# Cross attention: where four strip transposes, the scratch results and the values stand in PSUM and on TensorE's queue

## The reference

```python
q = _split_heads(query @ Wq.T + bq)
k = _split_heads(key @ Wk.T + bk)
v = _split_heads(value @ Wv.T + bv)
scores = jnp.einsum('bhqd,bhkd->bhqk', q, k) * scale
scores = jnp.where(mask == 0, NEG_INF, scores)
probs = jax.nn.softmax(scores, axis=-1)
out = jnp.einsum('bhqk,bhkd->bhqd', probs, v)
out = out.transpose(0, 2, 1, 3).reshape(query.shape[0], -1, D_MODEL)
return out @ Wo.T + bo
...
x = _layernorm(x + _L0_xattn_ref(x, ctx_1024, ctx_1024, mask_1x1xSxS2_ik0, ...), axis=-1)
```

## Time and profile before

| what | value |
|---|---|
| median of 3 executions | 491.06 us (490.84 to 491.5) |
| the profiled execution | 491.28 us |
| its span, first to last instruction | 489.5 us |
| TensorE matmuls busy | 439.8 us, 90% |
| TensorE weight loads busy | 308.6 us, 63% |
| VectorE busy | 248.3 us, 51% |
| ScalarE busy | 197.5 us, 40% |

### The profile page before, as it was taken

How to read it: one execution, slowest core, us unless ns; L and a number is a source line. 1 busy time by engine, 2 the same in 40 slices (tenths; PEclk the granted TensorE clock), 3 DMA queues, 4 the chain that set the end, 5 groups by cost and what they waited for, 6 DMA issues and landing times.

```text
span 489.5 us, 9697 instructions
## 1 busy us (share of the span) xinstructions
PE 439.8 (90%) x3440; PEld 308.6 (63%) x3441; DVE 248.3 (51%) x736; ACT 197.5 (40%) x582; POOL 42.4 (9%) x65
## 2 busy tenths in 40 slices
PE   5999999999999879999999999999879989999910
PEld 2797887977878646666666666666655646555500
DVE  0376465564655736566565655656644622222225
ACT  2235335243352426665565656566742110111200
POOL 3001011011010110001010101000000230000043
PEclk9999999999999989999999999999999999999975
DMA  7940000004200040404040406400000020111123
GB/s 282 307 192 1 11 1 11 11 0 161 73 1 2 1 161 0 153 11 149 14 161 1 162 2 248 172 0 2 4 1 1 23 75 0 32 43 43 37 65 103
DMA packets 15192, 33.28 MB, mean 68 GB/s; under 512 B 2128, under 2 KB 9536, under 8 KB 13760
## 3 DMA queue, kind: packets, MB, share of 16 engines
q1 hardware_dynamic: 14384, 30.91, 18.1%
q0 software_dynamic: 768, 1.84, 1.3%
HBM read 26.97 MB, written 5.77 MB: 67 GB/s over the span
## 4 chain that ended last, share of the span: by engine, by line
PE 75%; issue 8%; DVE 5%; ACT 5%; POOL 3%; DMA 3%; POOLq 0%; DVEq 0%; SPq 0%; ACTq 0%
PE bank L416 11%; PE bank L598 7%; PE bank L410 6%; PE bank L475 5%; PE bank L614 5%; PE bank L581 4%; PE bank L499 4%; PE bank L505 4%; PE bank L801 3%; ACT pT L947 3%; PE bank L825 3%; PE bank L807 3%; PE bank L433 3%; PE bank L461 3%; PE bank L734 3%
## 5 line engine op out<-in xcount | busy, mean ns | idle before, releaser
L1168 DVE CUSTOM_DVE_ANT_0 p<-bank,mask 112x375 f32<-112x375 f32 x128 | 63.6, 544 | 32.9 <-PE bank L581 32.1
L940 ACT ACTIVATE p<-p,nm 112x375 f32<-112x375 f32 x128 | 74.8, 606 | 9.7 <-DVE nm L1168 9.0
L598 PE MATMUL bank<-ident,p 112*125 112x112 f32 x384 | 61.1, 285 | 7.7 <-ACT pT L947 6.7
L598 PEld LDWEIGHTS bank<-ident,p 112*125 112x125 f32 x384 | 48.7, 188 | 29.7 <-issue 18.4
L416 PE MATMUL bank<-arena 128*128 128x112 f32 x512 | 61.9, 275 | 0.0
L947 ACT ACTIVATE pT<-bank 125x336 f32<-125x336 f32 x96 | 42.7, 446 | 46.7 <-PE bank L598 46.4
L416 PEld LDWEIGHTS bank<-arena 128*128 128x128 f32 x512 | 59.5, 192 | 0.5 <-issue 0.5
L884 ACT ACTIVATE arena<-bank,nm 112x112 f32<-112x112 f32 x128 | 43.5, 366 | 26.7 <-DVE nm L1043 26.7
L1036 DVE TENSOR_SCALAR arena<-bank 128x448 f32<-128x448 f32 x32 | 20.0, 624 | 41.1 <-PE bank L416 41.1
L410 PE MATMUL bank<-arena 128*112 128x512 f32 x64 | 32.6, 639 | 5.5 <-DMA arena<-in_wqkv 5.5
L892 ACT ACTIVATE arena<-bank 128x448 f32<-128x448 f32 x16 | 8.7, 543 | 58.6 <-PE bank L461 58.6
(11 more groups left out here) (136 smaller groups left out, 590.2 us busy)
## 6 DMA issues: line engine op xcount, KB each, us to landing
arena<-in_ug SPq DMA_DIRECT2D x8, 1024.0 KB, 6.0
arena<-in_dn SPq DMA_DIRECT2D x8, 512.0 KB, 6.9
mid<-in_ctxT SPq DMA_DIRECT2D x8, 375.0 KB, 3.1
arena<-in_wqkv SPq DMA_DIRECT2D x2, 1024.0 KB, 8.6
slots_x<-zeros SPq DMA_DIRECT2D x14, 128.0 KB, 1.8
xs<-slots_x SPq DMA_DIRECT2D x9, 128.0 KB, 2.0
slots_y<-p SPq DMA_DIRECT2D x9, 128.0 KB, 1.7
arena<-in_wqkv SPq DMA_DIRECT2D x2, 512.0 KB, 4.4
```

The source lines that it names most:

```text
L598: mm = pe.transpose(PE_T2[i % 2][0:SK, t * S:(t + 1) * S], p2[i % RING][:, t * SK:(t + 1) * SK], ident[0:S, 0:S])
L940: act.activation(p2[i % RING], p2[i % RING], ACT.Exp, bias=nm2[:, i % H:i % H + 1], scale=-1.0).then_inc(exp2, 1)
L1168: v.tensor_tensor_reduce(p2[i % RING], PE_S2[r][0:S, 0:S2], bias[:], 1.0, 3e38, ALU.add, ALU.min, accum_out=nm2[:, i % H:i % H + 1]).then_ ...
```

## The change

The transposed strips get four banks in place of two: strip 0 goes to bank 4, strip 1 to bank 7, strip 2 to bank 0 and strip 3 to bank 1. Banks 0 and 1 hold scores of the current slot, so these two wait for the minimum of the strip that was there (`max2`), and the next `score2` waits until both copies are made (`pt2_act`, `pt2_dve`). The scratch results of place 0 (x1's transposes, the queries, the output's two transposes) go to bank 6, in turn with the keys and the output projection; the waits that keep bank 6 apart are in `between`. The scratch results of place 1 go to bank 2 (`PE_L2`) behind the third minimum, and the first third of the next batch's values, before at place 2 in bank 6, joins them. `value2(n - 2)` moves behind `between(n, 2)` and so stands directly ahead of the next scores. In the end of the stage the last `value2` comes ahead of the router's first product.

```diff
-        PE_S2, PE_T2, PE_V2, PE_M2 = bank[0:STRIPS], (bank[4], bank[7]), bank[5], bank[6]
+        PE_S2, PE_V2, PE_M2 = bank[0:STRIPS], bank[5], bank[6]
+        PE_T2 = (bank[4], bank[7], PE_S2[0], PE_S2[1])
+        PE_L2 = PE_S2[2]
...
-            def turn_x1(b, M=PE_S2[0]):
+            def turn_x1(b, M=PE_M2):
...
-            def project_q(b, M=PE_S2[0]):
+            def project_q(b, M=PE_M2):
...
             def turn2_(n, r):
                 pe.wait_ge(exp2, n * STRIPS + r + 1)
-                if r >= 2:
-                    pe.wait_ge(pt2_act, n * 3 + r - 1)
-                elif n == 0:
+                if n == 0 and r < 2:
                     pe.wait_ge(y1, B)
                     pe.wait_ge(pt1, 4 * B)
                 elif r == 0:
-                    pe.wait_ge(pt2_act, n * 3)
-                else:
-                    pe.wait_ge(pt2_dve, n)
+                    pe.wait_ge(pt2_act, n * 3 - 2)
+                elif r == 1:
+                    pe.wait_ge(pt2_act, n * 3 - 1)
+                elif n + 1 < SLOTS:
+                    pe.wait_ge(max2, (n + 1) * STRIPS + r - 1)
...
-            def turn_o(b, M=PE_S2[0]):
+            def turn_o(b, M=PE_M2):
...
-            def turn_on(b, M=PE_S2[0]):
+            def turn_on(b, M=PE_M2):
...
-            def turn_x2(b, M=PE_S2[1]):
+            def turn_x2(b, M=PE_L2):
...
                 b, g = n // GROUPS, n % GROUPS
-                if place < 2:
-                    pe.wait_ge(max2, n * STRIPS + 1 + place)
+                if place == 1:
+                    pe.wait_ge(max2, n * STRIPS + 3)
                 if (g, place) == (0, 0) and b + 1 < B:
+                    if b == 0:
+                        pe.wait_ge(ot1[1], B)
+                    if b >= 2:
+                        pe.wait_ge(y2, b - 1)
                     turn_x1(b + 1)
                 if (g, place) == (0, 1) and b >= 1:
-                    project_v(2, b, PE_S2[1])
+                    project_v(2, b, PE_L2)
                 if (g, place) == (0, 2) and b + 1 < B:
-                    if b == 0:
-                        pe.wait_ge(ot1[1], B)
-                    elif b >= 2:
-                        pe.wait_ge(y2, b - 1)
+                    pe.wait_ge(x1t_sb, b + 2)
                     project_k(0, b + 1)
                 if (g, place) == (1, 0) and b + 1 < B:
+                    pe.wait_ge(k_sb, (b + 1) * KC + 1)
                     project_q(b + 1)
                 if (g, place) == (1, 1) and b >= 2:
                     turn_x2(b - 2)
                 if (g, place) == (1, 2) and b + 1 < B:
-                    pe.wait_ge(k_sb, (b + 1) * KC + 1)
+                    pe.wait_ge(q_sb, b + 2)
                     project_k(1, b + 1)
                 if (g, place) == (2, 0) and b >= 1:
+                    if b + 1 < B:
+                        pe.wait_ge(k_sb, (b + 2) * KC)
+                    else:
+                        pe.wait_ge(y2, B - 2)
                     turn_o(b - 1)
-                if (g, place) == (2, 2) and b + 1 < B:
-                    pe.wait_ge(k_sb, (b + 2) * KC)
-                    project_v(0, b + 1)
+                if (g, place) == (2, 1) and b + 1 < B:
+                    project_v(0, b + 1, PE_L2)
                 if (g, place) == (3, 0) and b >= 1:
                     turn_on(b - 1)
                 if (g, place) == (3, 1) and b + 1 < B:
-                    project_v(1, b + 1, PE_S2[1])
+                    project_v(1, b + 1, PE_L2)
                 if (g, place) == (3, 2) and b >= 1:
-                    if b + 1 < B:
-                        pe.wait_ge(v_sb, (b + 1) * KT + 1)
-                    else:
-                        pe.wait_ge(y2, B - 2)
                     out2(b - 1)
...
+                if n >= 2:
+                    pe.wait_ge(pt2_act, (n - 1) * 3)
+                    pe.wait_ge(pt2_dve, n - 1)
+                if g == 1 and b >= 1:
+                    pe.wait_ge(v_sb, b * KT + KT)
+                if g == 2 and b >= 2:
+                    pe.wait_ge(x2t_sb, b - 1)
+                if g == 3 and b + 1 < B:
+                    pe.wait_ge(v_sb, (b + 1) * KT + 1)
                 if g == 0 and b >= 1:
                     pe.wait_ge(v_sb, b * KT + 2)
...
                 between(n, 1)
+                between(n, 2)
                 if n >= 2:
                     value2(n - 2)
-                between(n, 2)
...
-            pe.wait_ge(ont_sb, B - 1)
+            value2(SLOTS - 1)
             logits_t(0, 4, bank[0])
-            value2(SLOTS - 1)
```

More of the change, by code:

```diff
@@ L592, in turn2_ @@
                 elif r == 0:
[L593 to L595 removed]
+                    pe.wait_ge(pt2_act, n * 3 - 2)
[3 more added lines that the diff above has]
+                    pe.wait_ge(max2, (n + 1) * STRIPS + r - 1)
                 i = n * STRIPS + r
                 for t in range(KT):
[L598 removed]
+                    mm = pe.transpose(PE_T2[r][0:SK, t * S:(t + 1) * S], p2[i % RING][:, t * SK:(t + 1) * SK], ident[0:S, 0:S])
                 mm.then_inc(turn2, 1)
@@ L682, in lent_banks_back @@
                 b, g = n // GROUPS, n % GROUPS
-                if g == 1:
-                    if b + 1 < B:
-                        pe.wait_ge(x1t_sb, b + 2)
-                    if b >= 1:
-                        pe.wait_ge(v_sb, b * KT + KT)
-                if g == 2:
-                    if b + 1 < B:
-                        pe.wait_ge(q_sb, b + 2)
-                    if b >= 2:
-                        pe.wait_ge(x2t_sb, b - 1)
-                if g == 3 and b >= 1:
-                    pe.wait_ge(on_sb, b)
+                if n >= 2:
[7 more added lines that the diff above has]
+                    pe.wait_ge(v_sb, (b + 1) * KT + 1)
                 if g == 0 and b >= 1:
                     pe.wait_ge(v_sb, b * KT + 2)
-                    if b >= 2:
-                        pe.wait_ge(ont_sb, b - 1)
             for n in range(SLOTS):
@@ L749, in _ @@
             pe.wait_ge(w_loaded["shared"], 32)
-            pe.wait_ge(ont_sb, B - 1)
+            value2(SLOTS - 1)
             logits_t(0, 4, bank[0])
-            value2(SLOTS - 1)
             pe.wait_ge(y2, B - 1)
-            turn_o(B - 1, PE_M2)
+            turn_o(B - 1)
             logits_t(4, 3, bank[1])
-            turn_on(B - 1, PE_M2)
+            turn_on(B - 1)
             shared(0, 0)
@@ L898, in evac_k, with evac_x1, evac_on, evac_x2 @@
                 act.activation(kT2[:, b % 2, m, :], J[:, 0:S2], ACT.Identity, bias=cols[:, 1, m:m + 1]).then_inc(k_sb, 1)
-            def evac_x1(b, M=PE_S2[0]):
+            def evac_x1(b, M=PE_M2):
                 act.wait_ge(x1t_pe, b + 1)
                 act.activation(x1T[:], M[:, 0:KC * S].rearrange("p (k n) -> p k n", k=KC), ACT.Copy).then_inc(x1t_sb, 1)
-            def evac_on(b, M=PE_S2[0]):
+            def evac_on(b, M=PE_M2):
                 act.wait_ge(ont_pe, b + 1)
                 act.activation(on2T[:], M[:, 0:KC * S].rearrange("p (k n) -> p k n", k=KC), ACT.Copy).then_inc(ont_sb, 1)
-            def evac_x2(b, M=PE_S2[1]):
+            def evac_x2(b, M=PE_L2):
                 act.wait_ge(x2t_pe, b + 1)
@@ L946, in evac_pt @@
                     act.wait_ge(pv2, n - 1)
-                act.activation(pT2[0:SK, i % RING], PE_T2[i % 2][0:SK, 0:KT * S].rearrange("p (k n) -> p k n", k=KT),
+                act.activation(pT2[0:SK, i % RING], PE_T2[r][0:SK, 0:KT * S].rearrange("p (k n) -> p k n", k=KT),
                                ACT.Copy).then_inc(pt2_act, 1)
@@ L997, in _ @@
             evac_logits(1, 0, 4, bank[0])
-            evac_on(B - 1, PE_M2)
+            evac_on(B - 1)
             evac_logits(2, 4, B - 1, bank[1])
@@ L1099, in query_scale, with evac_q @@
                 last.then_inc(prep, 1)
-            def evac_q(b, M=PE_S2[0]):
+            def evac_q(b, M=PE_M2):
                 v.wait_ge(q_pe, b + 1)
@@ L1175, in evac_pt2 @@
                     v.wait_ge(pv2, n - 1)
-                v.tensor_copy(pT2[0:SK, i % RING], PE_T2[i % 2][0:SK, 0:KT * S].rearrange("p (k n) -> p k n", k=KT)).then_inc(pt2_dve, 1)
+                v.tensor_copy(pT2[0:SK, i % RING], PE_T2[STRIPS - 1][0:SK, 0:KT * S].rearrange("p (k n) -> p k n", k=KT)).then_inc(pt2_dve, 1)
             def evac_ot(b):
@@ L1182, in evac_ot, with normalise2 @@
                 v.tensor_copy(oT2[:], PE_V2[:, 0:4 * S].rearrange("p (k n) -> p k n", k=4)).then_inc(ot2, 1)
-            def normalise2(b, M=PE_S2[0]):
+            def normalise2(b, M=PE_M2):
                 o = M[0:S, :].rearrange("p (h d) -> p h d", h=H)
@@ L1205, in between @@
                 if (g, place) == (0, 3) and b >= 1:
-                    evac_v(2, b, PE_S2[1])
+                    evac_v(2, b, PE_L2)
                 if (g, place) == (1, 0) and b >= 2:
@@ L1215, in between @@
                 if (g, place) == (2, 3) and b + 1 < B:
-                    evac_v(0, b + 1)
+                    evac_v(0, b + 1, PE_L2)
                 if (g, place) == (3, 3) and b + 1 < B:
```

(4 more changed lines are left out.)

1 line of the change is left out of this document (removed).

## The result

The changed kernel takes 483.53 us (median, 483.26 to 483.7) against 491.28 of the kernel before on the same chip: ratio 0.983, 95% interval 0.980 to 0.985. The profiled execution took 483.44 us with a span of 481.7, 7.8 less than the 489.5 of before. The prediction was 482.7.

A forecast was written before the change was run, and what follows sets the result against it. TensorE bounds the kernel, so only its idle time can be won. Five batches -6.6, first two batches -0.1, the end -0.9 and -0.8 sum to -8.4 us: 482.7 against 491.28, held between 480.5 and 486.

The forecast's parts named there:

- What bounds the kernel, and VectorE's frame: Cross attention: only TensorE's idle time is winnable; first minimum at +1.15, strips 0, 1, 2 known read at +1.76, +2.23, +2.70.
- Part 1: Place 0 scratch in bank 6 starts at +1.56 without a minimum; transposes 2, 3 use banks 0, 1; layernorm's 0.40 delay goes.
- Kinds 0, 1 and 3: Slots whose group is number 0, 1 or 3 in its batch; predicted to take 5.84, 5.78 and 5.35 us.
- Part 2: Scores wait for both strip copies; hidden by 0.7 or more in g = 0 and 3, exposed in g = 2.
- Kind 2: Slots of group 2 in a batch: a new 0.7 wait for a minimum, then VectorE's copy holds scores; 5.50 us.
- Part 3: Values moved directly ahead of scores: costed at nothing of itself as lower bound, up to +2.3 over 18 slots.
- First two batches: Stage start to slot 8's scores: keys 0.91 later for x1's copy, slots after that shorter; net -0.1 us.
- The end: Last batch to the sixth output projection -0.9 us; oT's copy under the router's product removes a TensorE wait, -0.8.
- Half of it: Rival: scores wait for VectorE's copies in g = 0 and 3 too, or values cost over 0.84; 486 to 488, chance 0.12.
- Nothing: Rival: the two new waits take back all 1.32 per batch if the first minimum starts 0.3 later; 491, chance 0.05.
- More than forecast: Rival: g = 2 slots find no wait and end at 4.8, 0.7 less per batch; 478 to 479, chance 0.02.
- The clock's rival: Idle time gathered in g = 2 lowers TensorE's granted clock, 1.7 us per fall; 494.6 with seven falls, chance 0.06.

The follow-up runs named there:

- values-back: Changed kernel with the values again ahead of place 2 (keys, output projection); ratio 0.9914 to the kernel before, 487.1 us by the ratio.
- kind 2 run: Changed kernel, g = 2 slots only: value projection behind the values in bank 6, VectorE's strip copy ahead of the bias; ratio 0.9719, 477.5 us by the ratio.
- copy-first: Changed kernel with VectorE's copy of the transposed strip ahead of the value bias in g = 2 slots only; ratio 0.9801, 481.5 us by the ratio.
- two-banks: Changed kernel with strips again in banks 4 and 7 and scores not waiting for their copies; ratio 0.9904, 486.6 us by the ratio.
- scratch-alone: Changed kernel with strips again in two banks and values ahead of place 2, keeping scratch placement and the new end order; ratio 1.0013 to the kernel before.

## Why the prediction was right, point by point

In terms of its sum, from the two traces:

| term | predicted | measured | from |
|---|---|---|---|
| scores of slot 0 to slot 8 | -0.1 | +1.0 | 45.02 to 46.06 |
| five batches | -6.6 | -7.0 | 118.96 to 111.93 |
| scores of slot 28 to the sixth output projection | -0.9 | -0.6 | 17.96 to 17.37 |
| x2's transposes to the output's transposes | -0.8 | -0.8 | 4.70 to 3.93 |
| ahead of the stage (-0.5), and all else (+0.1) | 0 | -0.4 | no edit there |
| sum | -8.4 | -7.8 | 489.5 to 481.7 |

The time came out 0.8 above the forecast (483.53 for 482.7), the sum of spans 0.6, and that closeness is partly luck: the first term missed by 1.1 and the end by 0.3, the batches gave 0.4 more than foretold, and another 0.4 came from where nothing was edited.

*What bounds the kernel, and VectorE's frame.* Right. The first minimum starts 1.15 after the scores in all kinds, also in g = 0 (only slot 19 has 1.49), and TensorE passes strips 2 and 3 and the lent bank near +1.85 and +2.7.

*Part 1.* Kinds 0, 1 and 3 came out at 5.73, 5.71 and 5.32 for 5.84, 5.78 and 5.35. The wait for q's copy is 0.26 on the weight load. The layernorm term was right in kind and size, and the values-back run shows it: 0.40 of g = 0 comes back with the old order.

*Part 2.* Kind 2 was 5.55 for 5.50: the minimum's wait 0.58 for 0.7, the copy's wait 0.26 for 0.3. The kind 2 and copy-first runs show that these two waits are most of what the slot loses, 0.84 of 0.97: without them and with the projection behind the values it takes 4.58, less than the 5.13 before the change.

*Part 3.* Mis-sized. The step put the move at nothing of itself, with costs only above. The values-back run gives 0.20 in g = 0 and 0.19 in g = 3 as a gain, and takes 0.14 back in g = 1. In the sum it shows where I had counted the keys at 1.46 as before: behind a projection and ahead of the values they took 1.36 (247.43 to 248.79), and g = 0 came out 0.11 shorter.

*First two batches.* The term that missed most, by 1.1. The 0.91 by which the keys come later was right (4.93 for 3.98 after the first scores, 0.95). The step then took the old low-clock durations, keys at 2.33 and only the scores slow in slot 1. It did not ask what a longer idle time does: in the profiled execution the keys took 2.77 to the scores, and the six transposes of slot 1 still ran slowly (1.54 for 0.91). With the gap filled, slots 0 and 1 are 2.65 shorter. But the size is not fixed either. Six profiled executions have the same slot 0 with the same idle time of 3.69 to 3.70 us: in the changed, values-back and copy-first runs slots 0 and 1 take 14.09, 14.00 and 14.36, in the two-banks, kind 2 and scratch-alone runs 13.06, 13.05 and 13.05, and the step's 13.0 is what the last three show. In the first three the stage begins at 175.4 to 175.8, in the last three at 177.0 to 177.1; whether that decides it was not tried.

*The end.* The slot of g = 1 in the last batch took 4.56 and not 4.36, and the projection came at +3.62 and not +3.53; the wait for oT's copy went away under the router's product, as said.

*The rivals.* "Half of it" did not come: the scores wait for VectorE's copy behind g = 2 and in the slots without other work (0.26 to 0.27), nowhere else. "Nothing" did not come either: it wanted a first minimum that starts 0.3 later than +1.15. "More than forecast" did not come in the changed kernel, but the kind 2 run shows that the slot can do without both waits. The clock's rival had the wrong place: in kind 2, with idle times of 0.58 and 0.26 inside 2 us, the granted clock is 1.00, and it is 1.00 in every stretch from 190 us to the end of the stage. The Trainium skill, page "TensorE: Matmul & The Clock Gate", section "A second HAM failure mode: psum-queue depth-cycling", tells of a kernel whose short idles between groups of matmuls, as it cycled through PSUM banks, made the clock swing; this trace does not agree with it for this rotation. The clock did move at the stage's first slot, where TensorE waits long once.

*The range.* Two of its figures do not follow from the working: Part 3's bound of +2.3 gives 485.0 and not 486 as the upper end, and 0.7 less in seven batches gives 477.8 and not 478 to 479. The result lies inside either way.

## What to carry to other kernels

When a strictly ordered queue waits at several places of a period, take the period kind by kind and ask at each which chain ends last: freeing one place (the scratch alone) moved its 0.6 us whole to the next wait, while the same edit together with the other two brought 1.7%. A bank that is borrowed from the next step's results makes the other engine's copy part of the period (0.26 us of the g = 2 slot here): before borrowing, look where in that engine's order the copy stands, and which piece waits for a bank although another bank is free. A single long wait of TensorE can go on costing after it: filling one of 3.69 us took 2.65 us off the work behind it.
